# Attention and feed-forward kernel: the value products of a head pair in two runs of 32 instead of four of 16, with PSUM banks and side work moved along

## The reference

```python
x = x + attn(layernorm(x))          # attn: layer norm again, gain gamma, then
q, k, v = xn @ Wq, xn @ Wk, xn @ Wv # 16 heads of width 64
q, k = rotary(q) / 8, rotary(k)
kt = einsum('bhnd,hde->bhne', k, W_bilinear)
sim = einsum('bhid,bhjd->bhij', q, kt)
out = softmax(sim) @ v              # 1024 x 1024 for each batch and head
x = x + (out @ Wo)
x = x + ffn(layernorm(x))           # ln, 256->1024 ternary weights, gelu, ln, 1024->256
```

## Time and profile before

| | us |
|---|---|
| median of three timed runs | 3471.37 |
| profiled execution, its own time | 3466.45 |
| span of its trace, first to last instruction | 3464.6 |
| PE busy | 3398.6 (98%) |
| DVE busy | 2636.0 (76%) |
| POOL busy | 2606.4 (75%) |
| ACT busy | 2313.3 (67%) |

### The profile page before, as it was taken

The page is one execution under the profiler, slowest core; times in us unless marked ns, Lnnn a source line. Parts: engine busy times, 40 slices in busy tenths (PEclk is TensorE's granted clock), DMA queues, the critical chain, the costliest instruction groups (busy, mean ns, idle before and its releaser), DMA issues. The chain is left out here.

```text
span 3464.6 us, 71914 instructions
## 1 busy us (share of the span) xinstructions
PE 3398.6 (98%) x21410; PEld 2200.6 (64%) x21410; DVE 2636.0 (76%) x4493; ACT 2313.3 (67%) x4412; POOL 2606.4 (75%) x1279
## 2 busy tenths in 40 slices
PE   6999999999999999999999999999999998899999
PEld 4655555555555555555555556566666664799998
DVE  6777777777777767777777777777777777899998
ACT  2666677666667766666766676677766666566665
POOL 2888888888889878888888888898888886122222
PEclk7999999999999999999999999999999999999999
DMA  5222323333323223332333333223322223333332
GB/s 197 83 88 95 119 94 102 102 123 102 102 92 117 98 98 102 118 102 96 99 123 102 102 102 119 96 94 100 118 90 93 75 74 113 101 100 100 102 105 69
DMA packets 255089, 355.75 MB, mean 103 GB/s; under 512 B 40220, under 2 KB 163484, under 8 KB 250268
## 3 DMA queue, kind: packets, MB, share of 16 engines
q1 hardware_dynamic: 245532, 343.29, 30.5%
q10 hardware_dynamic: 9216, 8.39, 0.7%
HBM read 219.49 MB, written 62.12 MB: 81 GB/s over the span
## 5 line engine op out<-in xcount | busy, mean ns | idle before, releaser
L463 POOL TENSOR_TENSOR prob_sum<-prob_sum,prob 128x1024 f32<-128x1024 f32 x762 | 1860.7, 2442 | 363.5 <-ACT prob L542 312.8
L542 ACT ACTIVATE prob<-scores 128x512 f32<-128x512 f32 x2048 | 1073.8, 600 | 525.8 <-PE scores L828 514.0
L752 DVE TENSOR_REDUCE row_max<-max_scores 128x1 f32<-128x512 f32 x1536 | 987.6, 684 | 428.0 <-PE max_scores L870 410.2
L1033 PE MATMUL attn_out<-prob,v 128*64 128x512 f32 x4096 | 934.3, 598 | 0.0
L819 PE MATMUL scores<-q_hi,k_hi 64*128 64x512 f32 x2048 | 785.5, 416 | 8.5 <-ACT prob L542 4.6
L824 PE MATMUL scores<-q_hi,k_lo 64*128 64x512 f32 x2048 | 755.5, 395 | 0.0
L828 PE MATMUL scores<-q_lo,k_hi 64*128 64x512 f32 x2048 | 751.8, 393 | 0.0
L1033 PEld LDWEIGHTS attn_out<-prob,v 128*64 128x64 f32 x4096 | 277.4, 137 | 565.3 <-issue 541.6
L870 PE MATMUL max_scores<-k_hi,q_hi 64*128 64x512 f32 x1536 | 578.9, 430 | 8.7 <-DVE row_max L752 5.5
L513 ACT ACTIVATE scores<-neg_max_seeds 128x512 f32<-128x512 f32 x1024 | 552.7, 598 | 42.7 <-DMA neg_max_seeds<-neg_max_halves 42.2
L819 PEld LDWEIGHTS scores<-q_hi,k_hi 64*128 64x128 f32 x2048 | 376.5, 185 | 284.0 <-issue 126.0
(11 more groups left out here) (148 smaller groups left out, 4771.9 us busy)
## 6 DMA issues: line engine op xcount, KB each, us to landing
rows<-rows SPq DMA_DIRECT2D x512, 128.0 KB, 2.0
neg_max_seeds<-neg_max_halves SPq DMA_DIRECT2D x128, 512.0 KB, 3.9
w_group<-w_parts SPq DMA_DIRECT2D x30, 1536.0 KB, 8.4
attn_normalised<-z_stage SPq DMA_DIRECT2D x128, 256.0 KB, 2.1
v<-attn_normalised SPq DMA_DIRECT2D x64, 512.0 KB, 4.1
sum_inverted_rows<-sums_inverted SPq DMA_DIRECT2D x126, 256.0 KB, 4.1
x_turned_parts<-x_tile_parts SPq DMA_DIRECT2D x49, 256.0 KB, 2.8
xt_batch<-x_turned_parts SPq DMA_DIRECT2D x7, 1792.0 KB, 10.3
```

The source lines that it names most:

```text
L463: nc.gpsimd.tensor_tensor(sums_of(k, half), a, prob[:, n % RING, :, :], ALU.add).then_inc(added, 1)
L542: nc.scalar.activation(prob[:, n % RING, e, :], S[e][n % 2][:, :], ACT.Exp).then_inc(exped[e], 1)
L752: nc.vector.reduce_max(mx[1 - u][:, e, n // 2, n % 2:n % 2 + 1], bank_of(e, jj)[:, :], axis=AX.X)\
L1033: nc.tensor.matmul(O[rows(e), :], V[k // 2 % 2][:, j, col:col + DH], prob[:, n % RING, e, :], start=j == 0, stop=j == 7).then_inc(pv_made[ ...
```

## The change

The value products of quarters 0 and 1 (blocks 0 to 7) are made together behind the burst of quarter 1, and those of quarters 2 and 3 (blocks 8 to 15) behind the bilinear keys of quarter 3: two runs of 32 matmuls in a span. Each run waits for a reduction first. `bank_of` takes the quarter into account: in quarter 1 the maxima's banks are O, M, X[1] in turn, in quarter 3 they are M, O, X[0]; quarters 0 and 2 keep X[0], X[1], M. The waits of `max_score` and of the keys follow. ACT's high parts of the input tile, DVE's `x_low` and `statistics` go from quarter 2 to 3, `norm_z` from quarter 0 to behind the reductions of quarter 1. On SP `max_seeds` and `sum_columns` go ahead of the z stores, and `store_x` goes behind `max_seeds` and `store_inverse`.

```diff
--- before.py
+++ after.py
@@ -264,9 +264,9 @@
         def has_tile(k):
             return k < T - PAIRS - 2
 
-        def bank_of(e, jj):
-
-            return (X[0], X[1], M)[MAX_ORDER.index((e, jj)) % 3]
+        def bank_of(e, jj, q):
+
+            return ((X[0], X[1], M), (O, M, X[1]), (X[0], X[1], M), (M, O, X[0]))[q][MAX_ORDER.index((e, jj)) % 3]
 
         def sums_of(k, half):
             return psums[(2 * k + half) % 3][:, :, :]
@@ -374,13 +374,13 @@
                 if proj:
                     for c in two:
                         swap(Q, t, c)
+                if attn:
+                    max_seeds(t - 1, 1)
+                if k >= 1:
+                    sum_columns(t - 1)
                 if k >= 2:
                     for h in two:
                         store_z(k - 2, t - 2, h)
-                if k >= 1:
-                    sum_columns(t - 1)
-                if attn:
-                    max_seeds(t - 1, 1)
                 if k == T - 2:
                     wait(sp, pv_made[1], 16 * t)
                     at_rest()
@@ -401,12 +401,12 @@
                     load_x(t + 1, k + 1, b + (k + 1) // PAIRS - k // PAIRS)
                 if prep:
                     max_rows(t, 0)
-                if proj and has_tile(k) and p != PAIRS - 1:
-                    store_x(t, k, b)
                 if prep:
                     max_seeds(t, 0)
                 if k >= 1:
                     store_inverse(t - 1)
+                if proj and has_tile(k) and p != PAIRS - 1:
+                    store_x(t, k, b)
                 if proj and p % 2 and k < T - 6:
                     wait(sp, v_made, 2 * (t + 2) + 2)
                     at_rest()
@@ -557,12 +557,6 @@
                         if has_tile(k):
                             wait(act, x_turned, t + 3)
                         max_row(t, 0)
-                    if q == 2 and has_tile(k):
-                        wait(act, x_turned, t + 3)
-                        wait(act, x_stored[u], 16 * ((t >> 1) + 1))
-                        for kt in range(KT):
-                            nc.scalar.activation(xparts[u][:, 0, kt, :], X[1][:, kt * P:(kt + 1) * P], ACT.Copy,
-                                                 scale=gam[:, kt:kt + 1]).then_inc(x_hi, 1)
                     if q == 0 and k >= 1:
                         copy_sums(t - 1)
                     if k == T - 2 and q == 3:
@@ -574,6 +568,12 @@
                         for shift, wide, tiles in ((shift1, wide1, KT), (shift2, wide2, HID // P)):
                             for i in range(tiles):
                                 nc.scalar.activation(wide[:, i, :], ones_full[:, :], ACT.Copy, scale=shift[:, i:i + 1]).then_inc(widened, 1)
+                    if q == 3 and has_tile(k):
+                        wait(act, x_turned, t + 3)
+                        wait(act, x_stored[u], 16 * ((t >> 1) + 1))
+                        for kt in range(KT):
+                            nc.scalar.activation(xparts[u][:, 0, kt, :], X[1][:, kt * P:(kt + 1) * P], ACT.Copy,
+                                                 scale=gam[:, kt:kt + 1]).then_inc(x_hi, 1)
                     if q == 3:
                         def keys(c):
                             wait(act, kt_made, 4 * (t + 2) + 2 * c + 2)
@@ -749,7 +749,7 @@
                         n = 4 * q + jj
                         if prep:
                             wait(dve, x_made[e], 16 * (t + 1) + n + 1)
-                            nc.vector.reduce_max(mx[1 - u][:, e, n // 2, n % 2:n % 2 + 1], bank_of(e, jj)[:, :], axis=AX.X)\
+                            nc.vector.reduce_max(mx[1 - u][:, e, n // 2, n % 2:n % 2 + 1], bank_of(e, jj, q)[:, :], axis=AX.X)\
                                 .then_inc(x_red[e], 1)
                     if q % 2 and prep:
                         negative(t, q // 2, 1 - u)
@@ -760,15 +760,15 @@
                             query_low(t - 1, 1 - u, 1)
                         if proj:
                             rotate(t, Q)
-                    if q == 0 and k >= 2:
-                        norm_z(k - 2, t - 2)
                     if q == 2 and k == -2:
                         constants()
                     if q == 1 and has_tile(k):
                         offset(t)
-                    if q == 2 and has_tile(k):
+                    if q == 1 and k >= 2:
+                        norm_z(k - 2, t - 2)
+                    if q == 3 and has_tile(k):
                         x_low(t, u)
-                    if q == 2 and has_tile(k + 1):
+                    if q == 3 and has_tile(k + 1):
                         statistics(t + 1, 1 - u)
                     if q == 2 and 1 <= k < T - 1:
                         invert(t - 1)
@@ -846,28 +846,38 @@
                     wait(pe, hi_made[Q], t + 2)
                     wait(pe, hi_made[K], 2 * (t + 1) + 2)
                     wait(pe, lo_made[K], 2 * (t + 1) + 2)
+                elif q == 0:
+                    if i == 1:
+                        wait(pe, nm_hi, 2 * t + 1)
+                        if has_tile(k - 1):
+                            wait(pe, x_lo, 2 * (t + 2))
+                elif q == 1:
+                    if i == 0:
+                        wait(pe, z_copied, 2 * t)
+                    elif i == 1:
+                        if proj:
+                            wait(pe, sin_made[Q], 2 * pp + 1)
+                        else:
+                            wait(pe, x_red[1], 16 * (t + 1) + 2)
+                    elif k >= 1:
+                        wait(pe, l_copied, t)
+                    elif attn:
+                        wait(pe, nm_hi, 2 * t + 2)
+                    else:
+                        wait(pe, x_red[1], 16 * (t + 1) + 4)
+                elif q == 2:
+                    if i == 0 and proj:
+                        wait(pe, sin_made[Q], 2 * pp + 2)
+                    else:
+                        wait(pe, x_red[1], 16 * (t + 1) + (3, 6, 8)[i])
                 elif i == 1:
-                    if q == 0 or q == 2:
-                        wait(pe, x_red[1], 16 * (t + 1) + 4 * q)
-                    elif q == 1:
-                        if k >= 1:
-                            wait(pe, l_copied, t)
-                        elif attn:
-                            wait(pe, nm_hi, 2 * t + 2)
-                        else:
-                            wait(pe, x_red[1], 16 * (t + 1) + 4)
-                    else:
-                        wait(pe, nm_hi, 2 * (t + 1) + 1)
-                        if has_tile(k):
-                            wait(pe, x_lo, 2 * (t + 3))
-                elif q == 1 and proj:
-                    wait(pe, sin_made[Q], 2 * pp + (2 if i == 0 else 1))
-                elif q == 3 and proj:
-                    wait(pe, v_copied, 2 * pp + (2 if i == 0 else 1))
-                elif q:
-                    wait(pe, x_red[1], 16 * (t + 1) + 4 * q - (1 if i == 0 else 2))
+                    wait(pe, z_copied, 2 * t + 1)
+                elif proj:
+                    wait(pe, v_copied, 2 * pp + (1 if i == 0 else 2))
+                else:
+                    wait(pe, x_red[1], 16 * (t + 1) + (10 if i == 0 else 11))
                 tile, part = n // 2, n % 2
-                nc.tensor.matmul(bank_of(e, jj)[:, :], QH[v][rows(e), tile * P:(tile + 1) * P], KH[v][rows(e), cols(part)],
+                nc.tensor.matmul(bank_of(e, jj, q)[:, :], QH[v][rows(e), tile * P:(tile + 1) * P], KH[v][rows(e), cols(part)],
                                  start=True, stop=True).then_inc(x_made[e], 1)
 
             def turn_max(t, h):
@@ -1004,9 +1014,9 @@
                                 if c == 0:
                                     if not prep:
                                         wait(pe, v_copied, 2 * pp + 1)
+                                    wait(pe, x_red[1], 16 * (t + 1) + 15)
+                                else:
                                     wait(pe, x_red[1], 16 * (t + 1) + 14)
-                                else:
-                                    wait(pe, x_red[1], 16 * (t + 1) + 15)
                                     if not prep:
                                         wait(pe, v_copied, 2 * pp + 2)
                                 for e in two:
@@ -1020,8 +1030,9 @@
                         if k == T - 1 and q == 3:
                             sums_last(0)
                         half = q // 2
-                        for jj in range(4):
-                            n = 4 * q + jj
+                        if q % 2 and prep:
+                            wait(pe, x_red[1], 16 * (t + 1) + (7 if q == 1 else 16))
+                        for n in range(8 * half, 8 * half + 8) if q % 2 else ():
                             j = n % 8
                             for e in two:
                                 if j == 0:
```

## The result

The changed kernel takes 3631.12 us (median of 4 runs, 3630.72 to 3632.57), against 3471.78 for the kernel before: a ratio of 1.0458, 95% interval 1.0440 to 1.0476. It is slower by 159 us. The forecast was 3634, the range of its own case 3600 to 3660, the whole range 3550 to 3685.

A forecast was written before the change was run, and what follows sets the result against it. PE was taken to bound the kernel; 2.39 + 0.63 + 0.05 - 0.30 - 0.14 = 2.63 us a span, 62 spans, +163 us on 3466.45, then 4.92: 3634 us. Own range 3600 to 3660 (chance 0.55), whole range 3550 to 3685.

The forecast's parts named there:

- Merging the runs: Value products: two runs of four go away, each saving 0.15 us of entering and leaving, 0.30 us a span.
- R: Time from burst 1's start to DVE's first reduction: 2.30 us, up from 1.48, as L732 waits for POOL's add.
- R + 4.65: Start of quarter 1's value products after burst 1's start, 4.56 before; a loss of 2.39 us a span.
- R + 0.75: When i = 3 of burst 1 may go, after bank O's reduction; PE would stand 1.4 us until then.
- The keys: Quarter 3's first keys product waits for the reduction of i = 6 in bank M: loss of 0.63 us a span.
- Burst 3 right behind the transposes: Its i = 0 wants bank M, from which ACT copied values: 0.05 us a span lost, bounds 0 and 0.2.
- SP and the seeds: max_seeds going ahead of z stores and sum columns on SP saves 0.14 us a span, bounds 0 and 0.68.
- The 4.92 us: Median of the runs above the profiled execution; added at the end, taking 3629 to 3634 us.
- At nothing: Side moves counted as free: x_low, statistics, ACT's x parts, store_x, and norm_z meeting POOL's adds.
- the rival of the late z chain: norm_z misses one more POOL add, copy_z and quarter 2's exponentials 1.4 us late: 3721 us; chance 0.17 with the clock.
- The rival of the earlier add: In quarter 0 L732 slips in behind an earlier POOL add, R stays 1.48: 3583 us; chance 0.23.
- the clock: TensorE's clock falls from the stops in burst 1, +93 us: 3727 us; chance 0.17 with the late z chain.

The follow-up runs named there:

- fourth kernel: Changed kernel with query_low of the second half moved a span earlier, and i = 6 of quarter 1 put into X[0] instead of O: 3521.23 us.
- tenth kernel: The seventh kernel with SP's old order (z stores, sum columns, then max_seeds): 3466.54 us, ratio 0.9984.
- third: Changed kernel with query_low of the second half (L732) moved from between quarter 0's rotations to the end of quarter 3, one span earlier: 3558.56 us.
- eighth kernel: Changed kernel with one more wait: POOL's add of block 3 waits until query_low of the second half is through: 3557.58 us.
- fifth: The fourth kernel with the keys' banks swapped, first half to X[0] and second to M: 3467.19 us, ratio 0.9983.
- seventh kernel: The second kernel with the banks of the keys' halves swapped: 3449.02 us, ratio 0.9926.
- first: Kernel before the change, with only SP's order changed, max_seeds and sum_columns ahead of the z stores: 3454.76 us, ratio 0.9944.
- ninth: Kernel before the change, unedited, profiled once more: 3475.4 us in a single execution.
- second kernel: Changed kernel with the merge in quarters 0 and 1 undone, blocks 8 to 15 still one run: 3494.19 us, ratio 1.0062.
- sixth kernel: The fifth kernel with quarter 1's banks in the order O, M, X[0], O, M, X[1], X[0], M: 3466.15 us, ratio 0.9979.

## Why the prediction was right

By its own steps:

- Merging the runs, 0.30 us a span saved: too much for the changed kernel. In the mean all value products of a span take 14.15 us, where they took 14.30. The run of quarter 1 took 7.11 us where 3.59 + 3.44 = 7.03 were in the sum; in the fourth kernel, where no wait stands ahead of it, PE's timeline has 7.02. So each merger is worth near 0.15 us as forecast, and about half of it is lost where PE comes to the run, or to the keys ahead of it, out of a standstill. The tenth kernel shows one merger, with its side moves, as a time: 7 us, 0.11 a span.
- R: 2.26 against 2.30 us, by the mechanism that was named (the third and, more sharply, the eighth kernel). In the span shown the value products of quarter 1 stood at 6.83 against R + 4.65 = 6.95. The difference is in two terms that were off in opposite senses: from i = 3 to i = 6 it took 2.47, not 2.72 us, and from the end of the reduction to the value products 0.24 (1521.97 to 1522.21), not 0.06. In the mean of the 62 spans burst 1 grew from 4.55 to 6.73, by 2.18 us, where the sum had 2.39.
- A detail that was missed: i = 1 goes into M, and waits for the first sine product. The prediction had PE run to i = 3 and stand there for 1.4 us; it stood 0.48 us at i = 1 and 0.59 at i = 3. The time up to i = 3 is the same, since i = 3 cannot go before R + 0.75 either way.
- The keys: 0.60 us of standstill, forecast 0.63; burst 3 grew from 4.49 to 5.18, by 0.69 us. The fifth and seventh kernel show that it goes when the banks are swapped.
- Burst 3 right behind the transposes, 0.05: in the seventh kernel, without the keys' stop, it takes 4.54 us against 4.49.
- SP and the seeds, 0.14 us a span between bounds of 0 and 0.68: between the two profiled executions it is as forecast, burst 2 fell from 4.65 to 4.50 us. As a time of the median run it is 17.5 to 20 us by the first and tenth kernel, 0.3 us a span. The one trace that the term was sized from had earlier seeds than the two others with SP's old order (burst 2 of 4.74 and 4.73 us in the ninth and tenth kernel).
- The 4.92 us between the profiled execution and the median of the runs, added at the end: the changed kernel has no such difference, its profiled execution took 3631.48 us and its median is 3631.12.
- At nothing: norm_z now meets POOL's adds (1.46 us for its first half at 1522.90, not 0.68) and nothing waits for it in PE's rows; store_x, x_low and statistics as said. So the rival of the late z chain (3721) did not come. That these cost nothing was only read from the traces, no kernel tested it alone. The end of the loop was at nothing without being named, and cost 9 us, 7.67 of them in one stop.

The rival of the earlier add (3583) was refuted by L732's 2.49 us (2.48 in the mean of 61 spans), the clock by the grant of 1.00 over the loop. The mechanism, the place and the order of size of both stops are as forecast, but the closeness of the total, 3 us, is in part luck. The 62 spans cost 156 us where the sum had 163, with burst 1 too long by 0.21 us a span and the gain of merging too large by 0.15; the end of the loop added 9 us that no term had, and the 4.92 us did not come.

## What to carry to other kernels

Before a block of matmuls is moved, list what it covered: here the 3.6 us of value products in quarter 0 hid a late VectorE, and a saving of 0.15 us uncovered over 2. When PSUM banks rotate, the last users of a bank set the wait of whoever takes it next, so give the next user the bank whose last use in the rotation is earliest; that alone was worth 45 us at the keys, from the second kernel to the seventh. The sixth kernel shows the limit: there the new bank had a late user of its own, and nothing was gained. Look at the ends of a loop too, where other work may have relied on the same cover: here one stop of 7.67 us. And split a change into its halves and its side moves: this one held an order of DMAs worth 17 us and a merger worth 7, under some 180 us of waits.

## What was not expected of the hardware

The wait itself was forecast: a VectorE instruction of 0.69 us with two SBUF inputs took 2.49 us in the changed kernel, since a GpSimd add had begun 0.47 us before it. What was not expected is the remedy: a wait put on GpSimd, one instruction long, made the kernel 74 us faster. And a DMA queue's order was worth more than its one profile showed: the wait for the seeds is 42.2 us in one execution of the same kernel and 52.4 in another. The sum of such a wait is no price, though: in the changed kernel it is 60.7 us and covered, since TensorE has a run of 7 us to do meanwhile.
